# Blending per-sample FFN weights in a fused attention and FFN layer: finer loads, two accumulators, and another place for the second weight matrix

## The chip, the cores and the metric

The kernel runs on 8 cores of one Trainium2 chip. There is no traffic between the cores: each takes one half (2048 positions of 4096) of one of four samples and its own copy of all weights. The time is device microseconds of the slowest core.

## The reference, cut to what matters

```python
xn = _layernorm(x)                       # x: (4, 4096, 1024)
x = x + attn(xn) + ffn(xn)               # windowed attention, 8 heads of 128, window 16

def _L0_ffn_ref(hidden_states, ...):     # F = 4096, H = 1024, E = 8
    h = relu(x @ gate_w1.T + gate_b1)
    g = (h @ gate_w2.T + gate_b2).mean(axis=1)              # (4, 8): one row a sample
    mW1 = W1 + einsum('be,efh->bfh', g, TW1)                # TW1: (8, 4096, 1024) f32
    mb1 = b1 + g @ Tb1
    mW2 = W2 + einsum('be,ehf->bhf', g, TW2)                # TW2: (8, 1024, 4096) f32
    mb2 = b2 + g @ Tb2
    u = gelu(einsum('bsh,bfh->bsf', x, mW1) + mb1)
    return einsum('bsf,bhf->bsh', u, mW2) + mb2
```

Each sample has its own blended weights. So each core adds eight float32 matrices of 16 MB, each times a scalar, to W1, and eight more to W2, before it can use either.

## The kernel before

Every instruction goes through small helpers of a class `Ctx` (so the profile gives one line for all matmuls, L74, one for all ACT operations, L85, one for all VectorE operations, L90, and one for all DMAs, L95). The program is written as one list of steps; each engine runs through it and keeps its own instructions in that order. `cx.wait_at(engine, semaphore, count)` makes one engine wait for a count that was noted when the awaited work was written; `cx.wait(engine, semaphores)` waits for everything on these semaphores written so far. DMAs are issued by the engine named in `cx.dma(q, ...)`, in the order in which they stand there, and a wait in front of a DMA holds up all that is behind it on that engine.

The steps, in order:

1. `emit_ln_gate` and `emit_g`: layer norm of all 4096 positions (written to `xnd` in HBM), the gate, and the eight blend factors `gbc`.
2. `emit_attn`: four chunks of 512 positions. A chunk starts with Q, K and V (`emit_qkv`), then has four tiles of 128 queries (`emit_attn_tile`). In a tile VectorE takes two reciprocals (`rz`), scales the probabilities (`exps`, `expsh`), and adds the residual (`xattn`, in the trace O_s<-pC and O_s<-pD); PE and ACT work in between, each in turn.
3. The builds (`emit_build_group`). Blended W1 (`m1d`) and W2 (`m2d`) are made in 64 groups of 128 rows x 1024: groups 0 to 31 are W1, 32 to 63 are W2. A group loads a 512 KB piece of W into the accumulator `accv` and eight 512 KB pieces of TW into `twv`, which has room for four. VectorE does eight multiply-adds (SCALAR_TENSOR_TENSOR) of 128x1024, the last of which writes bf16 into `mwov`, and a DMA takes that to HBM. TW comes in two transfers of four pieces (2 MB); the second overwrites the first, so it waits for the fourth multiply-add, and the next group's loads wait for the eighth. All of it is issued by SP. After each tile but the first stand three groups (line 533); the 19 that are left stand behind the attention (line 952).
4. `emit_ffn`: four chunks (`sc`) of 512 positions. In its first stage PE multiplies with blended W1 in eight blocks (`fb`), each loaded transposed from `m1d` by eight DMAs of SP, and ACT writes gelu to `u`. In its second stage it multiplies with blended W2 in 32 steps (`ft`), each with one transposed load from `m2d`. Before a block or a step SP waits until the groups that it needs are written (`wait_group_out`). The first matmul of the second stage has this line ahead of it:

```python
                if ft == 0:
                    cx.wait("tensor", "a", "v")
```

Of the kernel before, what the change touches and what calls it, by code (L numbers as in the profile page):

```python
# [10 lines left out]
F32 = mybir.dt.float32  # L11
BF16 = mybir.dt.bfloat16
AF = mybir.ActivationFunctionType
ALU = mybir.AluOpType
BF = ml_dtypes.bfloat16

B, T, D = 4, 4096, 1024
# [18 lines left out]
    "d_mb",  # L36
# [64 lines left out]
def build_program():  # L101
# [38 lines left out]
    s = {}  # L140
    for n, sh, dt in [
# [25 lines left out]
        ("accv", (128, D), F32), ("mwov", (128, D), BF16),  # L167
    ]:
# [45 lines left out]
    bk = {}  # L214
# [196 lines left out]
    def build_lane(g):  # L411
        return "vector"

    def emit_build_group(cx, g):
# [4 lines left out]
        osem = "d_mwo" if lane == "vector" else "d_mwop"
        oq = "sync" if lane == "vector" else "gpsimd"  # L420
        if g < 32:
# [21 lines left out]
        cx.dma(q, twb[:, 0:nper * D].rearrange("p (e d) -> p e d", d=D),
               twsrc[0:nper].rearrange("e f d -> f e d"), dsem)
        cx.wait_at(lane, "a", bk["gbc_a"])
        cx.wait(lane, dsem)
        for e in range(8):
            if e > 0 and e % nper == 0:
                cx.wait_at(q, eng_sem, cx.cnt[eng_sem])
                cx.dma(q, twb[:, 0:nper * D].rearrange("p (e d) -> p e d", d=D),  # L450
                       twsrc[e:e + nper].rearrange("e f d -> f e d"), dsem)
                cx.wait(lane, dsem)
            tw = twb[:, (e % nper) * D:((e % nper) + 1) * D]
            if e > 0:
                cx.wait(lane, "v" if lane == "vector" else "p")
            out = acc if e < 7 else outbuf
            if e == 7:
                po = bk["prev_out"].get(lane)
                if po is not None:
                    cx.wait_at(lane, osem, po)  # L460
            cx.vop("scalar_tensor_tensor", out, tw, s["gbc"][:, e:e + 1], acc,
                   op0=ALU.mult, op1=ALU.add, who=lane)
        bk["build_done"][g] = cx.cnt[eng_sem]
        bk["prev_lane"][lane] = g
        cx.wait_at(oq, eng_sem, bk["build_done"][g])
        cx.dma(oq, dst, outbuf, osem)
        bk["prev_out"][lane] = cx.cnt[osem]
        bk["group_out"][g] = (cx.cnt["d_mwo"], cx.cnt["d_mwop"])

    def emit_vector_builds(cx, n):  # L470
        done = 0
        g = bk["vq"]
        while done < n and g < 64:
            if build_lane(g) == "vector":
                emit_build_group(cx, g)
                done += 1
            g += 1
        bk["vq"] = g

    def emit_pool_builds(cx):  # L480
        for g in range(64):
            if build_lane(g) == "gpsimd":
                emit_build_group(cx, g)

    def emit_attn(cx):
# [4 lines left out]
        emit_pool_builds(cx)  # L490
        for ci in range(NCH):
# [28 lines left out]
            for j in range(NT):  # L520
# [11 lines left out]
                if gt >= 1:  # L532
                    emit_vector_builds(cx, 3)
# [240 lines left out]
    def emit_ffn(cx):  # L774
# [3 lines left out]
        for sc in range(NFC):  # L778
# [8 lines left out]
            for fb in range(8):  # L787
                bpar = fb % 2
# [31 lines left out]
            bk["xtf_war"] = cx.cnt["t"]  # L820
            banksets = [(pA, pB), (pC, pD), (pE0, pE1),
# [120 lines left out]
    def full_schedule(cx):  # L942
        emit_p0(cx)
        if PHASES >= 2:
            emit_ln_gate(cx)
        bk["pa_end_v"] = cx.cnt["v"]
        bk["pa_end_a"] = cx.cnt["a"]
        if PHASES >= 3:
            emit_g(cx)
        if PHASES >= 4:  # L950
            emit_attn(cx)
            emit_vector_builds(cx, 64)
        if PHASES >= 5:
            emit_ffn(cx)
            cx.wait("scalar", "d_out0", "d_out1")
        else:
            emit_dummy_out(cx)

    with nc.Block() as block:
        def run_for(name):  # L960
            def body(eng):
# [4 lines left out]
                    "build_done": {}, "prev_lane": {}, "prev_out": {}, "group_out": {},  # L966
# [111 lines left out]
```

How the kernel before makes its waits and increments, by code:

```python
    def inc(self, sname, instr, k=1):  # L57
        if instr is not None:
            instr.then_inc(self.sems[sname], k)
        self.cnt[sname] += k
# [1 line left out]
    def wait(self, who, *ss):  # L62
        if self.on(who):
            for sname in ss:
                if self.cnt[sname] > 0:
                    self.eng.wait_ge(self.sems[sname], self.cnt[sname])
# [1 line left out]
    def wait_at(self, who, sname, val):  # L68
        if self.on(who) and val > 0:
            self.eng.wait_ge(self.sems[sname], val)
```

## Time and profile before

| | us |
|---|---|
| median of 2 runs | 4000.21 (3997.89 to 4002.54) |
| the profiled execution, its own time | 4010.51 |
| its span on the slowest core (core 5) | 4008.7 |
| spans of the 8 cores | 3947.0 to 4008.7 |
| busy in the span: PE / VectorE (DVE) / ACT | 1178.3 / 971.2 / 365.9 |

No engine is busy for a third of the span. So the busy shares don't name what bounds the kernel, and the waits, the chain that ended last and the timeline have to. The span is cut by steps: 0 to 717 us are step 1 and the first Q, K and V, 717 to 2583 us attention tiles with their builds and three more rounds of Q, K and V, 2583 to 3160 us builds alone, and 3160 to 4009 us the FFN.

### The profile page before, as it was taken

What the parts mean: (1) busy time and instruction counts of PE and PEld (TensorE: products, weight loads), DVE (VectorE), ACT (ScalarE), POOL (GpSimd) and SP (SyncE); (2) the same over time, 40 slices, a digit from 0 to 9 for tenths busy, and PEclk for the clock granted to TensorE, in tenths of its full rate; (3) what the DMA queues carried; (4) which work ended last, traced back from release to release, by engine and by line L of the source; (5) the groups of instructions that cost most, each with busy time, mean ns of one, the idle gap of its engine ahead of it and who ended that gap; (6) DMA issues with size and microseconds to landing.
All of it is one profiled execution on the core that took longest, in us unless ns stands there. A gap on an engine that the chain in (4) does not pass through costs nothing.

```text
span 4008.7 us, 16002 instructions; the slowest of 8 cores (3947.0 to 4008.7 us)
## 1 busy us (share of the span) xinstructions
PE 1178.3 (29%) x5044; PEld 479.3 (12%) x5044; DVE 971.2 (24%) x943; ACT 365.9 (9%) x755; POOL 5.5 (0%) x11
## 2 busy tenths in 40 slices
PE   0433425411251112411134111000000175747475
PEld 0111102200020000200011000000000022213131
DVE  1111111344224442244422433333333200000000
ACT  0111102100120001200011000000000010102020
POOL 0000000000000000000000000000000000000000
PEclk9766768655675556755577555555555598888888
DMA  9132230145314442144521444444445445464644
GB/s 178 50 83 76 53 53 7 68 159 160 114 59 161 160 163 108 61 160 160 171 100 60 150 141 139 158 162 177 159 160 173 121 92 121 93 123 89 124 92 105
DMA packets 459878, 475.20 MB, mean 119 GB/s; under 512 B 356435, under 2 KB 356819, under 8 KB 459668
## 3 DMA queue, kind: packets, MB, share of 16 engines
q1 hardware_dynamic: 384996, 408.28, 33.6%
q10 hardware_dynamic: 70320, 55.40, 5.4%
q0 software_dynamic: 4480, 10.50, 1.7%
q8 instruction: 42, 0.69, 0.1%
q14 instruction: 40, 0.33, 0.0%
HBM read 357.91 MB, written 42.01 MB: 100 GB/s over the span
## 4 chain that ended last, share of the span: by engine, by line
DMA 36%; DVE 22%; PE 22%; SPq 6%; ACT 5%; issue 5%; ACTq 3%; DVEq 0%
DMA O_s<-TW 25%; DVE accv_s L90 14%; SPq L95 6%; DMA O_s<-m2d 6%; PE pA L74 5%; PE pB L74 4%; PE pC L74 4%; PE pU L74 3%; PE pD L74 3%; DVE rz_s L90 3%; ACTq L95 3%; PE pE L74 2%; DMA O_s<-xad 2%; DVE mwov_s L90 2%; DMA xnd<-xnb_s 1%
## 5 line engine op out<-in xcount | busy, mean ns | idle before, releaser
L90 DVE SCALAR_TENSOR_TENSOR accv_s<-O_s,gbc_s,accv_s 128x1024 f32<-128x1024 f32 x448 | 575.1, 1284 | 1102.2 <-DMA O_s<-TW 1068.1
L74 PE MATMUL pA<-O_s 128*128 128x512 bf16 x640 | 197.4, 430 | 965.8 <-DMA O_s<-m1d 758.0
L74 PE MATMUL pU<-rz_s,e0f_s 128*128 128x512 f32 x64 | 58.5, 1070 | 897.9 <-DVE rz_s L90 897.9
L74 PEld LDWEIGHTS pA<-O_s 128*128 128x128 bf16 x640 | 65.7, 106 | 1102.2 <-issue 1058.4
L90 DVE TENSOR_TENSOR O_s<-pA,O_s 128x512 f32<-128x512 f32 x4 | 2.8, 691 | 745.2 <-PE pU L74 745.2
L74 PE MATMUL pB<-O_s 128*128 128x512 bf16 x640 | 181.4, 400 | 0.0
L74 PEld LDWEIGHTS pU<-rz_s,e0f_s 128*128 128x128 f32 x64 | 18.8, 324 | 917.5 <-issue 917.5
L90 DVE RECIPROCAL rz_s<-pE 1x512 f32<-1x512 f32 x32 | 104.8, 3312 | 71.0 <-PE pE L74 71.0
L85 ACT ACTIVATE yt_s<-pU 128x128 bf16<-128x128 f32 x128 | 23.4, 305 | 1048.3 <-PE pU L74 1048.3
L74 PE MATMUL pC<-gb1r_s,e0bf_s 128*128 128x512 bf16 x32 | 13.9, 435 | 350.0 <-DMA xt_s<-xnd 343.2
L90 DVE TENSOR_SCALAR_CACHE_REDUCE junk_s<-O_s 128x1024 f32<-128x1024 f32 x32 | 38.8, 1214 | 319.9 <-ACT hrelu_s L85 319.4
L74 PE MATMUL pE<-O_s 128*128 128x512 bf16 (+1 forms) x384 | 108.4, 337 | 0.0
L85 ACT ACTIVATE O_s<-pA,mb_s 128x512 bf16<-128x512 f32 x64 | 44.0, 687 | 539.2 <-PE pA L74 539.2
L74 PE MATMUL pA<-xt_s,O_s 128*128 128x512 bf16 (+1 forms) x288 | 71.0, 394 | 50.9 <-DMA xt_s<-xnd 44.3
L90 DVE SCALAR_TENSOR_TENSOR mwov_s<-O_s,gbc_s,accv_s 128x1024 bf16<-128x1024 f32 x64 | 82.2, 1285 | 11.0 <-DVE accv_s L90 10.9
L74 PE MATMUL pC<-O_s,xt_s 128*128 128x512 bf16 x256 | 78.6, 462 | 0.0
L74 PE MATMUL pA<-O_s,selbf_s 128*32 128x512 bf16 x15 | 6.4, 428 | 244.7 <-DVE O_s L90 244.7
L74 PE MATMUL pU<-O_s 128*128 128x512 bf16 x256 | 78.3, 388 | 0.0
L74 PEld LDWEIGHTS pB<-O_s 128*128 128x128 bf16 x640 | 66.3, 104 | 75.8 <-issue 23.7
L85 ACT ACT_TABLE_LOAD x2 | 2.6, 1283 | 742.5 <-PE pA L74 696.4
L74 PE MATMUL pC<-O_s,yt_s 128*128 128x512 bf16 x128 | 56.7, 623 | 27.3 <-ACT yt_s L85 27.3
L74 PE MATMUL pD<-O_s 128*128 128x512 bf16 (+1 forms) x192 | 64.6, 336 | 0.0
(135 smaller groups left out, 1335.5 us busy)
## 6 DMA issues: line engine op xcount, KB each, us to landing
O_s<-TW SPq DMA_DIRECT2D x128, 2048.0 KB, 8.5
accv_s<-W SPq DMA_DIRECT2D x64, 512.0 KB, 4.1
O_s<-x SPq DMA_DIRECT2D x16, 1024.0 KB, 7.1
xnd<-xnb_s ACTq DMA_DIRECT2D x32, 256.0 KB, 3.6
O_s<-x ACTq DMA_DIRECT2D x16, 512.0 KB, 3.8
xad<-O_s ACTq DMA_DIRECT2D x16, 512.0 KB, 3.0
m1d<-mwov_s SPq DMA_DIRECT2D x32, 256.0 KB, 2.2
m2d<-mwov_s SPq DMA_DIRECT2D x32, 256.0 KB, 3.4
```

What stands on the lines that cost most here:

```text
L74: i = self.eng.matmul(out, lhsT, rhs, start=start, stop=stop, skip_group_check=skip)
L85: i = self.eng.activation(out, in_, func, **kw) if self.on("scalar") else None
L90: i = getattr(self.eng, name)(*args, **kw) if self.on(who) else None
L95: i = self.eng.dma_start(out=out, in_=in_, transpose=transpose)
```

## The change

- There are four slots for TW, each with a semaphore of its own (`d_ts0` to `d_ts3`). TW comes in eight transfers of 512 KB, one a slot; the load of a slot waits only for the multiply-add that read the slot last. Each multiply-add waits for its own slot.
- There are two accumulators and two output buffers (`accv2` and `mwov2` are new), taken in turn. The load of W waits for the last group but one.
- The write of a group is issued behind its loads and ahead of the next group's, after the eighth multiply-add, on the same engine.
- Behind each tile stand two groups instead of three, and only of W1: 30 in all. The last two of W1 stand in the first FFN chunk ahead of its blocks 0 and 1. All 32 of W2 stand between the first and the second stage of that chunk, and their DMAs are issued by ACT, not SP. They go by columns first: all eight row blocks of one quarter of the columns, then the next quarter.

```diff
+    BLD_ORDER = list(range(32)) + [32 + ht * 4 + fq
+                                   for fq in range(4) for ht in range(8)]
...
     def emit_build_group(cx, g):
...
+        m1 = g < 32
+        q = "sync" if m1 else "scalar"
...
-        prevg = bk["prev_lane"].get(lane)
-        if prevg is not None:
-            cx.wait_at(q, eng_sem, bk["build_done"][prevg])
...
-        cx.dma(q, acc, wsrc, dsem)
-        cx.dma(q, twb[:, 0:nper * D].rearrange("p (e d) -> p e d", d=D),
-               twsrc[0:nper].rearrange("e f d -> f e d"), dsem)
-        cx.wait_at(lane, "a", bk["gbc_a"])
-        cx.wait(lane, dsem)
+        par = bk["bld_n"] % 2
+        acc = s["accv"] if par == 0 else s["accv2"]
+        outbuf = s["mwov"] if par == 0 else s["mwov2"]
+        wdsem = "d_tw" if par == 0 else "d_twp"
+        osem = "d_mwo" if par == 0 else "d_mwop"
+        slots = [s["twv"][:, r * D:(r + 1) * D] for r in range(4)]
+        cx.wait_at(q, "v", bk["acc_done"][par])
+        cx.dma(q, acc, wsrc, wdsem)
...
         for e in range(8):
-            if e > 0 and e % nper == 0:
-                cx.wait_at(q, eng_sem, cx.cnt[eng_sem])
-                cx.dma(q, twb[:, 0:nper * D].rearrange("p (e d) -> p e d", d=D),
-                       twsrc[e:e + nper].rearrange("e f d -> f e d"), dsem)
-                cx.wait(lane, dsem)
...
+            i = i0 + e
+            r = i % 4
...
+            elif e < 4:
+                cx.wait_at(q, "v", bk["mac_cnt"][i - 4])
+            else:
+                cx.wait_at(q, "v", v0 + (e - 4) + 1)
+            ssem = "d_ts%d" % r
+            cx.dma(q, slots[r], twsrc[e], ssem)
+            bk["slot_dma"][i] = (ssem, cx.cnt[ssem])
+        for e in range(8):
+            i = i0 + e
+            ds, dc = bk["slot_dma"][i]
+            cx.wait_at("vector", ds, dc)
...
+            cx.vop("scalar_tensor_tensor", out, slots[i % 4],
+                   s["gbc"][:, e:e + 1], acc, op0=ALU.mult, op1=ALU.add)
...
+        cx.wait_at(q, "v", done)
+        cx.dma(q, dst, outbuf, osem)
...
                 if gt >= 1:
-                    emit_vector_builds(cx, 3)
+                    emit_vector_builds(cx, 2, only_m1=True)
...
             for fb in range(8):
+                if sc == 0:
+                    emit_vector_builds(cx, 1, only_m1=True)
                 bpar = fb % 2
...
             bk["xtf_war"] = cx.cnt["t"]
+            if sc == 0:
+                emit_vector_builds(cx, 64)
             banksets = [(pA, pB), (pC, pD), (pE0, pE1),
...
             emit_attn(cx)
-            emit_vector_builds(cx, 64)
         if PHASES >= 5:
             emit_ffn(cx)
```

What SP issues for the first builds before the change (accv is the accumulator, O_s<-TW a load into the slots, m1d<-mwov_s the write of a group of W1; "waits v" is a wait for VectorE):

```order
L95 DMA m2row_s<-mbd 1x1024 [waits d_mb]
L95 DMA accv_s<-W 128x1024 [waits v,a]
L95 DMA O_s<-TW 128x4x1024
L95 DMA O_s<-TW 128x4x1024 [waits v]
L95 DMA m1d<-mwov_s 128x1024 [waits v]
L95 DMA accv_s<-W 128x1024 [waits v]
L95 DMA O_s<-TW 128x4x1024
```

And after it:

```order
L95 DMA m2row_s<-mbd 1x1024 [waits d_mb]
L95 DMA accv_s<-W 128x1024
L95 DMA O_s<-TW 128x1024 [waits v,a] x4
L95 DMA O_s<-TW 128x1024 [waits v] x4
L95 DMA m1d<-mwov_s 128x1024 [waits v]
L95 DMA accv_s<-W 128x1024
L95 DMA O_s<-TW 128x1024 [waits v] x8
L95 DMA m1d<-mwov_s 128x1024 [waits v]
```

The two transfers of 2 MB have become eight of 512 KB with a wait for each, and the write of a group still stands, with its wait for VectorE, ahead of all loads of the next.

What ACT has at the end of the first stage of the first FFN chunk before the change (O_s<-pA,mb_s is a gelu, O_s<-xad the load of the attention's result for the last addition):

```order
L85 ACTIVATE O_s<-pB,mb_s 128x512 [waits t]
L85 ACTIVATE O_s<-pA,mb_s 128x512 [waits t]
L85 ACTIVATE O_s<-pB,mb_s 128x512 [waits t]
L95 DMA O_s<-xad 128x1024 [waits d_xa0,v]
L95 DMA out<-O_s 128x1024 [waits v]
```

And after it:

```order
L85 ACTIVATE O_s<-pA,mb_s 128x512 [waits t]
L85 ACTIVATE O_s<-pB,mb_s 128x512 [waits t]
L95 DMA accv_s<-W 128x1024 [waits v]
L95 DMA O_s<-TW 128x1024 [waits v] x8
L95 DMA m2d<-mwov_s 128x1024 [waits v]
L95 DMA accv_s<-W 128x1024 [waits v]
L95 DMA O_s<-TW 128x1024 [waits v] x8
```

The loads of W2's 32 groups stand behind the last gelu of the chunk's first stage, and ahead of the loads for its last addition.

What SP has after the change between the last write of the attention's builds and the second block of the first FFN chunk (O_s<-xnd is the transposed input, O_s<-m1d a block of blended W1):

```order
L95 DMA m1d<-mwov_s 128x1024 [waits v]
L95 DMA_TRANSPOSE O_s<-xnd 128x512 [waits t]
L95 DMA_TRANSPOSE O_s<-xnd 128x512 x7
L95 DMA accv_s<-W 128x1024 [waits v]
L95 DMA O_s<-TW 128x1024 [waits v] x8
L95 DMA m1d<-mwov_s 128x1024 [waits v]
L95 DMA_TRANSPOSE O_s<-m1d 128x512 [waits d_mwo,d_mwop,t]
L95 DMA_TRANSPOSE O_s<-m1d 128x512 x7
L95 DMA accv_s<-W 128x1024 [waits v]
L95 DMA O_s<-TW 128x1024 [waits v] x8
L95 DMA m1d<-mwov_s 128x1024 [waits v]
L95 DMA_TRANSPOSE O_s<-m1d 128x512 [waits d_mwo,d_mwop]
```

Before, all builds had been issued by then, and the rows O_s<-m1d stood right behind O_s<-xnd. Now one group stands ahead of the first block and one ahead of the second.

PE's order is the same in both. Its first matmul of the second stage waits for `v` and `a` as counted at that point of the program; after the change the 32 groups of W2 are counted there too:

```order
L74 MATMUL pB<-O_s 128x512 [waits a]
L74 MATMUL pB<-O_s 128x512 x7
L74 MATMUL pA<-m2rowb_s,e0bf_s 128x512 [waits d_m20,a,v]
L74 MATMUL pB<-m2rowb_s,e0bf_s 128x512
L74 MATMUL pC<-m2rowb_s,e0bf_s 128x512
```

## Rows read from the trace of the kernel before

**Rows 1.** The page: span, chain that ended last by engine and by line.

```profile
span 4008.7 us, 16002 instructions; the slowest of 8 cores (3947.0 to 4008.7 us)
...
DMA 36%; DVE 22%; PE 22%; SPq 6%; ACT 5%; issue 5%; ACTq 3%; DVEq 0%
DMA O_s<-TW 25%; DVE accv_s L90 14%; SPq L95 6%; DMA O_s<-m2d 6%; PE pA L74 5%; PE pB L74 4%; PE pC L74 4%; PE pU L74 3%; PE pD L74 3%; DVE rz_s L90 3%; ACTq L95 3%; PE pE L74 2%; DMA O_s<-xad 2%; DVE mwov_s L90 2%; DMA xnd<-xnb_s 1%
```

**Rows 2.** Busy time in stretches of the span: us, busy by engine, PEclk, DMA share, GB/s.

```profile
core 5: us, PE busy (x) PEld busy (x) DVE busy (x) ACT busy (x) POOL busy (x), PEclk, DMA share, GB/s
...
717.00:1046.00 329.00, 60.31 (x264) 27.00 (x262) 128.12 (x100) 15.13 (x50) 0.00 (x0) 0.57 0.40 141
...
2583.00:3160.00 577.00, 0.00 (x0) 0.00 (x0) 195.33 (x153) 0.00 (x0) 0.00 (x0) 0.50 0.47 164
3160.00:3376.00 216.00, 130.82 (x520) 51.40 (x520) 2.58 (x4) 23.27 (x33) 0.00 (x0) 0.86 0.49 98
```

**Rows 3.** Timeline of one attention tile: start us, us, engine, line, operation.

```profile
1350.81 6.55 DVE L90 RECIPROCAL rz_s<-pE 1x512 f32<-1x512 f32 x2
...
1373.44 0.68 DVE L90 TENSOR_TENSOR O_s<-pD,O_s 128x512 f32<-128x512 f32 x1
1374.04 5.44 DVE L90 SCALAR_TENSOR_TENSOR accv_s<-O_s,gbc_s,accv_s 128x1024 f32<-128x1024 f32 x4
...
1379.56 0.38 SPq L95 DMA_DIRECT2D O_s<-TW  x1
...
1381.60 0.31 PE L74 MATMUL pE<-expsh_s,ohalbf_s 128*1 128x128 bf16 x1
1387.76 4.06 DVE L90 SCALAR_TENSOR_TENSOR accv_s<-O_s,gbc_s,accv_s 128x1024 f32<-128x1024 f32 x3 [8.28 <-DMA O_s<-TW]
1392.00 1.28 DVE L90 SCALAR_TENSOR_TENSOR mwov_s<-O_s,gbc_s,accv_s 128x1024 bf16<-128x1024 f32 x1 [0.17 <-DVE accv_s L90]
1393.36 0.36 SPq L95 DMA_DIRECT2D m1d<-mwov_s  x1
...
1394.24 14.92 SPq L95 DMA_DIRECT2D O_s<-TW  x2
1403.25 5.45 DVE L90 SCALAR_TENSOR_TENSOR accv_s<-O_s,gbc_s,accv_s 128x1024 f32<-128x1024 f32 x4 [9.97 <-DMA O_s<-TW]
```

**Rows 4.** Groups of VectorE instructions from 770 to 2584 us: the 45 groups beside attention.

```profile
L90 DVE SCALAR_TENSOR_TENSOR accv_s<-O_s,gbc_s,accv_s 128x1024 f32<-128x1024 f32 x315 | 404.3, 1284 | 724.0 <-DMA O_s<-TW 699.7 <-DVE accv_s L90 0.9
...
L90 DVE SCALAR_TENSOR_TENSOR mwov_s<-O_s,gbc_s,accv_s 128x1024 bf16<-128x1024 f32 x45 | 57.8, 1285 | 7.7 <-DVE accv_s L90 7.6
```

**Rows 5.** The chain that ended last, in order of time: start us, us, what.

```profile
2408.12 14.43 DMA O_s<-TW
2428.17 10.45 DMA O_s<-TW
...
2977.38 10.54 DMA O_s<-TW
2993.54 8.20 DMA O_s<-TW
```

**Rows 6.** The page's DMA issues: KB each, median us from issue to landing.

```profile
O_s<-x ACTq DMA_DIRECT2D x16, 512.0 KB, 3.8
```

**Rows 7.** Timeline of the start of the FFN, PE and SP.

```profile
3160.41 10.13 SPq L95 DMA_TRANSPOSE O_s<-xnd  x8
3170.70 87.57 SPq L95 DMA_TRANSPOSE O_s<-m1d  x64
3184.34 3.57 PE L74 MATMUL pA<-O_s 128*128 128x512 bf16 x8 [686.49 <-DMA O_s<-m1d]
...
3206.77 3.57 PE L74 MATMUL pA<-O_s 128*128 128x512 bf16 x8 [5.79 <-DMA O_s<-m1d]
...
3217.96 1.89 PE L74 MATMUL pA<-O_s 128*128 128x512 bf16 x8 [2.42 <-DMA O_s<-m1d]
...
3268.60 0.38 PE L74 MATMUL pA<-m2rowb_s,e0bf_s 128*128 128x512 bf16 x1 [1.14 <-ACT O_s L85]
```

More of the change, by code:

```diff
@@ L35 @@
     "d_xr0", "d_xr1", "d_xa0", "d_xa1", "d_xf0", "d_xf1", "d_out0", "d_out1",
-    "d_mb",
[1 row of a table added]
     "t", "v", "a", "p",
@@ L167, in build_program @@
         ("accv", (128, D), F32), ("mwov", (128, D), BF16),
+        ("accv2", (128, D), F32), ("mwov2", (128, D), BF16),
     ]:
@@ L445, in emit_build_group @@
-        cx.wait_at(lane, "a", bk["gbc_a"])
-        cx.wait(lane, dsem)
-        for e in range(8):
-            if e > 0 and e % nper == 0:
-                cx.wait_at(q, eng_sem, cx.cnt[eng_sem])
-                cx.dma(q, twb[:, 0:nper * D].rearrange("p (e d) -> p e d", d=D),
-                       twsrc[e:e + nper].rearrange("e f d -> f e d"), dsem)
-                cx.wait(lane, dsem)
-            tw = twb[:, (e % nper) * D:((e % nper) + 1) * D]
-            if e > 0:
-                cx.wait(lane, "v" if lane == "vector" else "p")
-            out = acc if e < 7 else outbuf
[L457 to L462, printed above, removed]
@@ new lines, in emit_build_group @@
+        cx.wait_at(q, "v", bk["acc_done"][par])
+        cx.dma(q, acc, wsrc, wdsem)
+        wsem, wcnt = wdsem, cx.cnt[wdsem]
+        i0 = bk["bld_idx"]
+        v0 = cx.cnt["v"]
+        for e in range(8):
+            i = i0 + e
+            r = i % 4
+            if i < 4:
+                cx.wait_at(q, "v", bk["pa_end_v"])
+                cx.wait_at(q, "a", bk["pa_end_a"])
+            elif e < 4:
[5 more added lines that the diff above has]
+            bk["slot_dma"][i] = (ssem, cx.cnt[ssem])
@@ new lines, in emit_build_group @@
+        for e in range(8):
+            i = i0 + e
+            ds, dc = bk["slot_dma"][i]
+            cx.wait_at("vector", ds, dc)
+            if e == 0:
+                cx.wait_at("vector", wsem, wcnt)
+                cx.wait_at("vector", "a", bk["gbc_a"])
+            cx.wait("vector", "v")
+            out = acc if e < 7 else outbuf
+            if e == 7 and bk["out_sem"][par] is not None:
+                osm, ocn = bk["out_sem"][par]
+                cx.wait_at("vector", osm, ocn)
+            cx.vop("scalar_tensor_tensor", out, slots[i % 4],
+                   s["gbc"][:, e:e + 1], acc, op0=ALU.mult, op1=ALU.add)
+            bk["mac_cnt"][i] = cx.cnt["v"]
@@ L468, in emit_build_group, with emit_vector_builds @@
+        bk["bld_idx"] = i0 + 8
+        done = cx.cnt["v"]
+        bk["acc_done"][par] = done
+        cx.wait_at(q, "v", done)
+        cx.dma(q, dst, outbuf, osem)
+        bk["out_sem"][par] = (osem, cx.cnt[osem])
+        bk["bld_n"] += 1
         bk["group_out"][g] = (cx.cnt["d_mwo"], cx.cnt["d_mwop"])
-    def emit_vector_builds(cx, n):
+    def emit_vector_builds(cx, n, only_m1=False):
         done = 0
[L472 to L483, printed above, removed]
+        while done < n and bk["vq"] < 64:
+            if only_m1 and BLD_ORDER[bk["vq"]] >= 32:
+                return
+            emit_build_group(cx, BLD_ORDER[bk["vq"]])
+            bk["vq"] += 1
+            done += 1
     def emit_attn(cx):
@@ L489, in emit_attn @@
         bk["kt_war"] = bk["g_done_t"]
-        emit_pool_builds(cx)
         for ci in range(NCH):
@@ L965, in body @@
                     "relu_a": [], "hbar_t": [], "xt_gate_t": [],
-                    "build_done": {}, "prev_lane": {}, "prev_out": {}, "group_out": {},
+                    "group_out": {},
+                    "bld_n": 0, "bld_idx": 0, "slot_dma": {}, "mac_cnt": {},
+                    "acc_done": {0: 0, 1: 0}, "out_sem": {0: None, 1: None},
                     "vq": 0, "hraw_a": [], "qraw_a": [], "kstt_v": [], "ppa": [],
```

22 lines of the change are left out of this document (1 added, 21 removed), and 1 row of the table SEM_NAMES.

## The prediction

> **What bounds the kernel now.** I read the page first. The chain that ended last is 36% DMA and 22% VectorE; its two longest entries are the loads of TW, 25%, and the multiply-adds on the accumulator, 14% [rows 1]. That is the build of the blended weights. The stretches then show where it stands alone: from 2583 to 3160 us PE and ACT do nothing, VectorE is busy 195 of 577 us and the DMA engines 0.47 of the time at 164 GB/s [rows 2]. So neither engine is full; they take turns. The timeline shows how. The first four multiply-adds end at 1379.5, the next load goes out at 1379.56, VectorE idles 8.28 us, works 5.5 us, the write goes out at 1393.36, and the next multiply-add starts at 1403.25 [rows 3]. A group of W1 is 9.9 + 5.5 + 8.3 + 5.5, some 29.3 us, of which 11 are work. In the stretch with builds alone, all W2, it is 577 / 19 = 30.4.
>
> Attention does not cover this. A tile's own part, from the reciprocals at 1350.81 to the residual at 1374.04, needs VectorE in between and takes 23.2 us [rows 3]. PE has the next tile ready at about 1381.9, 8 us later, and waits for VectorE, which has builds for another 70. So each group's time is added to the tile's. The 45 groups in attention cost 404.3 + 724.0 + 57.8 + 7.7 = 1193.8 us, busy and idle together [rows 4]: 79.6 a tile, less than three times 29.3 since the first group's loads land during the tile's own part. The last 19 cost 577 us. Together 1771 of 4010.5 us.
>
> **A group after the change.** The write still stands between two groups on the issuing engine, behind the wait for the eighth multiply-add. So four slots are not refilled across the border: at each border nothing is in flight, and write, W and four TW loads go out together, with the same bytes as now. They land as now: 9.9 us from the write's issue to the fourth slot [rows 3]. The gain is behind that. The fifth load goes out when the first multiply-add is done, long before the fourth slot lands, and comes right behind it in the stream. A load of 512 KB takes 3.8 us [rows 6], one of 2 MB 7.8 us (1379.56 to 1387.76, less the waits for semaphores and the start) [rows 3]: the three further pieces cost 1.33 us each. After that VectorE sets the pace. Today multiply-adds stand 1.39 us apart with one wait, and 1.46 us where there are two (three take 4.06 us, the one after them starts 4.24 us after the first; 4.24 - 2 x 1.39) [rows 3]; now all have two. So a group of W1 is 9.9 + 1.3 + 4 x 1.46 = 17.1 us, and one of W2 1.1 more (30.4 - 29.3), 18.2.
>
> The rate is the doubtful part, since each core will ask for 280 GB/s where it asked for 164. The first bound is 1.33 us a slot. The other comes from 164 GB/s at a DMA share of 0.47 [rows 2]: full engines would move 349 GB/s, 1.50 us for 512 KB. I take the middle, 1.41. Six slots' worth of bytes stand in a row at a border, so 6 x 0.09, some 0.55 us a group: 17.65 for W1 and 18.75 for W2.
>
> Here a page speaks. The Trainium skill, HBM Reference, Specifications, says that two cores share a memory stack, a core alone reaches some 425 GB/s and each of two about 358. By that an estimate is 1.46 us a slot when both stream, and the sum below would be some 15 us higher. No row here shows one core against its neighbour.
>
> The first group of a tile finds W and four pieces landed, as now (four multiply-adds follow 1374.04 at once) [rows 3]. Its fifth piece goes out after the first multiply-add and lands 3.8 us later, when the fourth ends. So it is 8 x 1.46 = 11.7 us. The 23.2 us of the tile's own part cover the 9.9 us; without that cover it would be 17.65.
>
> **The parts of the sum.**
> - Attention: 15 tiles x (11.7 + 17.65) = 440 us instead of 1193.8: -753.5. The next tile is ready 8 us after the builds begin, so 29 us of builds still hide that. The 23.2 us and the three rounds of Q, K and V stay. I give nothing for a warmer PE: its granted clock is 0.57 in these stretches [rows 2] since it idles for some 70 us in every tile, and it would still idle 20 us; after a gap of only 5.79 us it has fallen to the lower level (8 matmuls in 3.57 us), after 2.42 us it has not (1.89 us) [rows 7].
> - The last two groups of W1: on SP they stand behind the transposed input (10.3 us) and ahead of blocks 0 and 1. Now the first block comes 23.9 us after 3160.41, of which 13.6 from its own issue [rows 7]. After: 10.3 + 17.2 + 0.45 + 13.6 = 41.6, 17.7 later. Behind the block's eight issues (10 us) comes the second group and then block 1: 28 + 10 + 17.65 + 13.6 = 69.3, against 46.4 now. Queued behind is only SP's own list; PE and ACT wait for it. Together +23.
> - W2: 32 groups x 18.75 = 600 us instead of the 577 us of the 19 that stood alone: +23. They start when ACT has issued its last gelu. Nothing lies beside them. Their order by columns suggests that the second stage should overlap with them, but its first matmul waits for VectorE's count with all 32 in it, where it now waits only for a gelu (idle 1.14 us at 3268.60) [rows 7]. Behind them on ACT's queue are the loads for the last addition, which are not due yet.
> - The second accumulator and output buffer: nothing. The write is behind the wait for the group's end in any case, and W's load lands ahead of the first slot. No instruction is added but the issues, 0.38 us each [rows 3], six more a group; they run under the transfers.
> - The rest of the FFN stays: three chunks and the second stage of the first.
>
> 4010.5 - 753.5 + 23 + 23 = 3303 us against the profiled execution. That one is 10 us above the median of the runs, 4000.2, so I take 8 off: **3295 us**, -17.6%. A microsecond a group is worth 15 + 2 + 32 = 49 us.
>
> **Rivals.**
> - *The loads stream at full rate across the whole group.* If the fixed part of a landing overlapped even at the border, a group would be its 4.98 MB at 349 GB/s, 14.3 us: 15 x 26 = 390, 32 x 14.3 = 458, the two of W1 +16, in all 4010.5 - 804 - 119 + 16 = 3103. For it: the DMA engines have room. Against: the write and its wait in front of all loads of the next group, in the order of the program.
> - *The memory gives out.* Between 2408 and 2439 us two transfers took 14.43 and 10.45 us instead of 10.54 and 8.20 [rows 5], at less than half load. At that price throughout, 5.5 + 2.6 more than the 8.9 and 7.8 of rows 3, a group of W1 would be 25 us, the sum 3666. Half of that extra, 4 us a group, gives 3470. For it: all eight cores now read harder, W2 in pieces of rows far apart. Against: later transfers of the same kind are short again.
> - *Small loads are paid singly* (this is the one that ends above the time before). If each of the nine loads cost its 3.8 us [rows 6] with no overlap with the one ahead on the queue, a group would be 0.4 + 9 x 3.8 + 1.5 = 36.1 us and the first of a tile 18.2: 15 x 54.3 = 815, 32 x 36.1 = 1155, +60 for the two of W1, 4010.5 - 379 + 578 + 60 = 4270 us. It becomes slower by 2% from 32.4 us a group. Against it: write, W and the 2 MB behind them are all issued between 1393.36 and 1394.24 and have landed by 1403.25, 9.9 us; W and the 2 MB singly would be 3.8 + 7.8 = 11.6 without the write [rows 3, 6].
> - *The second stage does overlap with W2.* Then three quarters of some 100 us (3268.60 to 3376) go: 3220. The wait named above speaks against it.
>
> A page speaks for the third rival. The Trainium skill, DMA: Bandwidth & Descriptors, Measured, asks for transfers of at least 1 MiB, and puts a single one at 2.0 us and its bytes at 436 GB/s; its estimate for 512 KB is 3.2 us. Paid singly, that makes 30.7 us a group and a time of about 4005, no gain. The same page says that the fixed part is mostly the wait for completion, which need not hold up the next transfer, and the row on W and the 2 MB agrees.
>
> **How the numbers follow.** Forecast (groups of 16.5 to 19.5 us, 3230 to 3380): 0.62. Memory gives out: 0.19. Full stream: 0.12. Overlap of the second stage: 0.03. Small loads singly: 0.04, half of it above +2%. The range reaches to the full stream and to half the extra of the slow transfers: 3110 to 3480. Within 2% is what a measurement of this kernel can hardly tell from no change; only the third rival and halves of it get there. Faster 0.97, same 0.01, slower 0.02.
>
> **What would show it.** After the change: groups behind the first of a tile 17 to 18 us from write to write, with VectorE idle some 6 us before the first multiply-add and then 1.3 to 1.5 us between starts; first groups 11 to 12 us; a tile 52 to 53 us from reciprocal to reciprocal instead of 99; W2's groups about 600 us with PE idle all through; PE's first matmul of the second stage released by VectorE; the FFN's last three chunks as before. I am wrong if landing times of single slots climb with load (then W2's groups show it first), if VectorE idles before each multiply-add rather than at borders, or if PE has matmuls between W2's groups.

## The result and the profile after

The changed kernel takes 3491.6 us (median of 11 runs, 3482.07 to 3508.78) against 4000.0 (10 runs): a ratio of 0.873, 95% interval 0.871 to 0.875. A few executions of any kernel here are some per cent slow on one half of the chip; the ratios, and the medians of the experiments below, leave those out. The forecast was 3295, with a range from 3110 to 3480. The direction, what bounds the kernel and where the gain lies were right; the saving is 508 us instead of 705, and the time lies 12 us above the range.

The page of the kernel after, its span and the chain that ended last, by engine and line (the answer to [rows 1]), and its loads (the answer to [rows 6]: KB each, median us from issue to landing):

```profile
span 3495.8 us, 17506 instructions; the slowest of 8 cores (3407.8 to 3495.8 us)
...
DMA 34%; PE 26%; DVE 18%; ACT 6%; issue 6%; SPq 6%; ACTq 4%; DVEq 1%
DMA O_s<-TW 21%; DVE accv_s L90 9%; DMA O_s<-m2d 6%; PE pA L74 6%; SPq L95 6%; PE pB L74 5%; PE pC L74 5%; PE pU L74 4%; ACTq L95 4%; PE pD L74 4%; DVE rz_s L90 3%; PE pE L74 2%; DMA O_s<-xad 2%; DVE mwov_s L90 2%; DMA xnd<-xnb_s 2%
...
O_s<-TW SPq DMA_DIRECT2D x256, 512.0 KB, 5.8
O_s<-TW ACTq DMA_DIRECT2D x256, 512.0 KB, 6.9
accv_s<-W SPq DMA_DIRECT2D x32, 512.0 KB, 4.1
accv_s<-W ACTq DMA_DIRECT2D x32, 512.0 KB, 5.5
...
O_s<-x ACTq DMA_DIRECT2D x16, 512.0 KB, 4.0
```

The loads of TW are still the largest entry. A single 512 KB transfer that stands alone, O_s<-x, takes 4.0 us, against 3.8 before. The same amount as a slot's load takes 5.8 us for W1 (SP's queue) and 6.9 us for W2 (ACT's).

One tile with its two groups of W1, VectorE and SP (the answer to [rows 3]):

```profile
1069.26 6.55 DVE L90 RECIPROCAL rz_s<-pE 1x512 f32<-1x512 f32 x2
...
1092.10 0.68 DVE L90 TENSOR_TENSOR O_s<-pD,O_s 128x512 f32<-128x512 f32 x1
1092.89 5.45 DVE L90 SCALAR_TENSOR_TENSOR accv_s<-O_s,gbc_s,accv_s 128x1024 f32<-128x1024 f32 x4
1099.53 1.28 DVE L90 SCALAR_TENSOR_TENSOR accv_s<-O_s,gbc_s,accv_s 128x1024 f32<-128x1024 f32 x1 [1.19 <-DMA O_s<-TW]
1101.72 1.28 DVE L90 SCALAR_TENSOR_TENSOR accv_s<-O_s,gbc_s,accv_s 128x1024 f32<-128x1024 f32 x1 [0.91 <-DMA O_s<-TW]
1103.74 1.28 DVE L90 SCALAR_TENSOR_TENSOR accv_s<-O_s,gbc_s,accv_s 128x1024 f32<-128x1024 f32 x1 [0.74 <-DMA O_s<-TW]
1105.20 1.28 DVE L90 SCALAR_TENSOR_TENSOR mwov_s<-O_s,gbc_s,accv_s 128x1024 bf16<-128x1024 f32 x1 [0.17 <-DVE accv_s L90]
1106.56 0.34 SPq L95 DMA_DIRECT2D m1d<-mwov_s  x1
...
1107.47 12.31 SPq L95 DMA_DIRECT2D O_s<-TW  x8
1113.92 5.45 DVE L90 SCALAR_TENSOR_TENSOR accv_s<-O_s,gbc_s,accv_s 128x1024 f32<-128x1024 f32 x4 [7.44 <-DMA O_s<-TW]
1119.70 1.28 DVE L90 SCALAR_TENSOR_TENSOR accv_s<-O_s,gbc_s,accv_s 128x1024 f32<-128x1024 f32 x1 [0.33 <-DMA O_s<-TW]
...
1125.31 1.28 DVE L90 SCALAR_TENSOR_TENSOR mwov_s<-O_s,gbc_s,accv_s 128x1024 bf16<-128x1024 f32 x1 [0.17 <-DVE accv_s L90]
1126.51 6.55 DVE L90 RECIPROCAL rz_s<-pE 1x512 f32<-1x512 f32 x2
```

The shape is the one in the prediction. The first group of the tile starts at once with four multiply-adds; then the fifth piece is late by 1.2 us, and the group ends 13.7 us after its start instead of 11.7 (1092.89 to the write at 1106.56). At the border the write goes out at 1106.56 and the next multiply-add starts at 1113.92, 7.4 us later, and the fifth at 1119.70, 13.1 us after the write instead of 11.2. The whole second group is 20.1 us, from 1106.56 to the write at 1126.66. The tile is 57.3 us where 52 to 53 were expected.

The groups of VectorE instructions over the whole of attention's builds (the answer to [rows 4]), 30 groups:

```profile
L90 DVE SCALAR_TENSOR_TENSOR accv_s<-O_s,gbc_s,accv_s 128x1024 f32<-128x1024 f32 x210 | 269.7, 1284 | 185.5 <-DMA O_s<-TW 171.2 <-DVE accv_s L90 0.5
...
L90 DVE SCALAR_TENSOR_TENSOR mwov_s<-O_s,gbc_s,accv_s 128x1024 bf16<-128x1024 f32 x30 | 38.5, 1285 | 7.6 <-DVE accv_s L90 3.9 <-DMA O_s<-TW 3.6
```

Busy and idle together make 501 us, 33.4 a tile, where 440 us were forecast.

A group of W2, from the write before it:

```profile
2318.15 0.35 ACTq L95 DMA_DIRECT2D m2d<-mwov_s  x1
...
2319.07 12.53 ACTq L95 DMA_DIRECT2D O_s<-TW  x8
2325.73 5.45 DVE L90 SCALAR_TENSOR_TENSOR accv_s<-O_s,gbc_s,accv_s 128x1024 f32<-128x1024 f32 x4 [7.66 <-DMA O_s<-TW]
2332.77 1.28 DVE L90 SCALAR_TENSOR_TENSOR accv_s<-O_s,gbc_s,accv_s 128x1024 f32<-128x1024 f32 x1 [1.58 <-DMA O_s<-TW]
2335.20 1.28 DVE L90 SCALAR_TENSOR_TENSOR accv_s<-O_s,gbc_s,accv_s 128x1024 f32<-128x1024 f32 x1 [1.15 <-DMA O_s<-TW]
2336.91 1.28 DVE L90 SCALAR_TENSOR_TENSOR accv_s<-O_s,gbc_s,accv_s 128x1024 f32<-128x1024 f32 x1 [0.43 <-DMA O_s<-TW]
2338.37 1.28 DVE L90 SCALAR_TENSOR_TENSOR mwov_s<-O_s,gbc_s,accv_s 128x1024 bf16<-128x1024 f32 x1 [0.17 <-DVE accv_s L90]
2339.74 0.35 ACTq L95 DMA_DIRECT2D m2d<-mwov_s  x1
```

The fifth load can go out when the first multiply-add ends, 2327.0, and its multiply-add starts at 2332.77, 5.8 us later. I had given 3.8 us to that load. That is one half of what a group costs too much; the other lies at the border. Averaged over 28 of W2's groups on this core (timeline, 2060 to 2740 us), VectorE idles 8.4 us between the last multiply-add of a group and the first of the next, where some 6 were forecast, and takes 13.9 us from there to the group's end, where 8 x 1.46 = 11.7 were. At the end of these groups PE starts, released by VectorE, as the wait for its count says:

```profile
2752.22 0.59 PE L74 MATMUL pA<-m2rowb_s,e0bf_s 128*128 128x512 bf16 x1 [708.51 <-DVE mwov_s L90]
```

### The profile page after: what moved, and what is told of

Same layout as the page of the kernel before. It is cut to its first block, busy times and chain, and to the rows that moved or that the text cites. A ratio compares the mean times of both kernels' runs of the same rounds, so it can differ in the third digit from the quotient of the medians.

```text
span 3495.8 us, 17506 instructions; the slowest of 8 cores (3407.8 to 3495.8 us)
## 1 busy us (share of the span) xinstructions
PE 1206.6 (35%) x5044; PEld 487.1 (14%) x5044; DVE 972.7 (28%) x943; ACT 365.9 (10%) x755; POOL 5.5 (0%) x11
## 4 chain that ended last, share of the span: by engine, by line
DMA 34%; PE 26%; DVE 18%; ACT 6%; issue 6%; SPq 6%; ACTq 4%; DVEq 1%
DMA O_s<-TW 21%; DVE accv_s L90 9%; DMA O_s<-m2d 6%; PE pA L74 6%; SPq L95 6%; PE pB L74 5%; PE pC L74 5%; PE pU L74 4%; ACTq L95 4%; PE pD L74 4%; DVE rz_s L90 3%; PE pE L74 2%; DMA O_s<-xad 2%; DVE mwov_s L90 2%; DMA xnd<-xnb_s 2%
## 5 line engine op out<-in xcount | busy, mean ns | idle before, releaser
L74 PE MATMUL pC<-gb1r_s,e0bf_s 128*128 128x512 bf16 x32 | 14.3, 448 | 342.5 <-DMA xt_s<-xnd 335.7
L74 PE MATMUL pC<-O_s,xt_s 128*128 128x512 bf16 x256 | 85.7, 495 | 0.0
L74 PEld LDWEIGHTS pU<-rz_s,e0f_s 128*128 128x128 f32 x64 | 18.8, 324 | 401.1 <-issue 401.1
L90 DVE SCALAR_TENSOR_TENSOR O_s<-raw_s,qwc_s,rbq_s 128x512 bf16<-128x512 f32 x32 | 21.6, 746 | 163.7 <-ACT rbq_s L85 163.7
```

What stands on the lines that cost most here:

```text
L74: i = self.eng.matmul(out, lhsT, rhs, start=start, stop=stop, skip_group_check=skip)
L90: i = getattr(self.eng, name)(*args, **kw) if self.on(who) else None
```

## The experiments

The price of a group below is read from one view: a stretch in which VectorE does nothing but multiply-adds, its length divided by the count in brackets behind VectorE's busy time, times eight. The columns are the stretch, its length, busy time (x count) of PE, PE's weight loads, VectorE, ACT and POOL, the granted clock, the DMA share and GB/s. For the kernel before it is the row 2583:3160 of [rows 2]: 577 / 153 x 8 = 30.2 us, DMA share 0.47 at 164 GB/s. For the kernel after, W2's groups, 600 / 216 x 8 = 22.2 us:

```profile
2100.00:2700.00 600.00, 0.00 (x0) 0.00 (x0) 275.17 (x216) 0.00 (x0) 0.00 (x0) 0.50 0.73 224
```

All of these rows are of the slowest core of their run. The same view on the other cores of this execution gives 20.7 us on cores 0 and 1 and 21.5 to 22.2 on the rest, so a few tenths between two runs mean little.

My theory at this point ("load"): the slots' landings grow because other cores read at the same time. The rival ("singly"): each 512 KB transfer costs something on its own queue, whoever else reads.

### One core, two cores

The edit, for the kernel after and for the kernel before (2 in the place of 1 for two cores); the cores that don't run leave their part of the output to a copy of core 0's or 1's:

```diff
+    in_maps = in_maps[:1]
-    res = run_bass_kernel_spmd(nc, in_maps, core_ids=list(range(8)))
+    res = run_bass_kernel_spmd(nc, in_maps, core_ids=list(range(1)))
...
-        out[b, t * OWN:(t + 1) * OWN] = np.asarray(res.results[core]["out"])
+        out[b, t * OWN:(t + 1) * OWN] = np.asarray(res.results[core % 1]["out"])
```

The changed kernel on one core:

> The changed kernel on one core, seven cores idle; the output of that core stands for all. Theory 'load': a slot lands late because the other cores read at the same time. Then TW's median landing on ACT's queue falls from 6.9 us to 5 or less, a group of W2 from 22.1 to 17 to 18.5 us, and the span to about 3300 us. Theory 'singly': each 512 KB transfer pays something of its own on its queue, whoever else reads. Then landing 6.5 to 7, groups 21 to 22 us, span 3440 or more.

On two cores:

> The changed kernel on two cores, 0 and 1. If neighbours share what is short, groups of W2 are as slow as with eight cores (21 to 22 us, span 3400 to 3490). If what is short is shared by the whole chip, they are as fast as with one core (17 to 18.5 us, about 3300). Theory 'singly': no difference between one, two and eight.

The kernel before on one core:

> The kernel before on one core. Theory 'load': half as hard a reader gains less: a group of W2 goes from 30.4 to 28 to 29 us, landing of 2 MB from 8.5 to 8, span 3880 to 3940. Theory 'singly': unchanged, 3980 to 4010.

Measured: 3314.6 us on one core, 3511.7 on two, 3491.6 on eight. The kernel before on one core: 3921.6. The page's DMA issues of the changed kernel on one core:

```profile
O_s<-TW SPq DMA_DIRECT2D x256, 512.0 KB, 5.1
O_s<-TW ACTq DMA_DIRECT2D x256, 512.0 KB, 5.5
```

ACT's slots land after 5.5 us instead of 6.9, not after 5 or less as the theory had it. The lone load O_s<-x takes 3.5 us on this core, so more than half of what a slot's load takes beyond a lone one is there without any neighbour. W2's groups with one core, then with two, then the kernel before with one:

```profile
2050.00:2600.00 550.00, 0.00 (x0) 0.00 (x0) 290.76 (x227) 0.00 (x0) 0.00 (x0) 0.50 0.75 257
```

```profile
2100.00:2740.00 640.00, 0.00 (x0) 0.00 (x0) 294.96 (x231) 0.00 (x0) 0.00 (x0) 0.50 0.74 226
```

```profile
2560.00:3100.00 540.00, 0.00 (x0) 0.00 (x0) 184.86 (x144) 0.00 (x0) 0.00 (x0) 0.50 0.48 165
```

A group of W2 costs 19.4 us with one core, 22.2 with two (22.4 on core 0) and 20.7 to 22.2 with eight. The one-core figure misses the 17 to 18.5 that was expected, and 3511.7 us lies above the 3490. But the whole rise from 19.4 comes with the first neighbour, and the six other cores add nothing that shows: cores 0 and 1 share what is short. "Singly" falls as the cause of that rise, though not of the 19.4 itself. Why the same pair paid 22.2 to 22.4 in one execution and 20.7 in the other stays open, and no run puts core 0 beside a core that is not its neighbour.

For core 0, alone and with core 1, the timelines give by stage: 39 us more to the end of attention (1851.7 to 1890.3), 92 us more for W2's 32 groups (617 to 709), 32 us more behind them (699 to 731). So of the 168 us between the two spans (3312.9 and 3481.3) somewhat over half is W2's groups, and the neighbour costs something in every stage. The kernel before is 2% faster when alone, but its groups of W2 are 540 / 144 x 8 = 30.0 us there against 30.2, where I had expected 28 to 29, and its 2 MB transfers land after 8.5 us in both: it waits for one transfer at a time, and a neighbour hardly mattered in that stretch. What it gains lies elsewhere, and part of it is only that core 0 is set against the slowest of eight: core 0 itself had a span of 3947.0 us in the profiled execution before, 27 more than the 3919.8 alone, and 24 of these lie ahead of its first tile (reciprocals at 710.4 and 686.6 us).

The Trainium skill, HBM Reference, Specifications, says that the two cores of a pair share one memory stack. The pattern of one, two and eight cores (19.4, 22.2, 20.7 to 22.2 us) agrees.

### The new loads alone, the new places alone

`slots_only` has the new loads in the old places:

```diff
-        q = "sync" if m1 else "scalar"
+        q = "sync"
...
-    BLD_ORDER = list(range(32)) + [32 + ht * 4 + fq
-                                   for fq in range(4) for ht in range(8)]
+    BLD_ORDER = list(range(64))
...
-                    emit_vector_builds(cx, 2, only_m1=True)
+                    emit_vector_builds(cx, 3)
...
-                if sc == 0:
-                    emit_vector_builds(cx, 1, only_m1=True)
...
-            if sc == 0:
-                emit_vector_builds(cx, 64)
...
             emit_attn(cx)
+            emit_vector_builds(cx, 64)
```

> The new loads (four slots, two accumulators) in the old places: three groups a tile, 19 behind the attention, all issued by SP, rows of W2 in the old order. By the prices of the changed kernel's profile (first group of a tile 13.6 us, a further one 20 us, W2 22 us): 45 groups in attention 15 x (13.6 + 40.2) = 807 instead of 1194, 19 groups 420 instead of 577, so about 3460 to 3490 us, level with the changed kernel: the move is worth nothing. Rival: ACT's queue or the order by columns makes W2 slow; then the 19 groups take 20 us or less each and the whole 3400 to 3440.

`move_only` has the new places with the old loads and one accumulator:

```diff
-        cx.dma(q, acc, wsrc, wdsem)
...
-            cx.dma(q, slots[r], twsrc[e], ssem)
...
+        cx.dma(q, acc, wsrc, "d_tw")
+        cx.dma(q, twb[:, 0:nper * D].rearrange("p (e d) -> p e d", d=D),
+               twsrc[0:nper].rearrange("e f d -> f e d"), "d_tw")
...
+            if e == nper:
+                cx.wait_at(q, "v", cx.cnt["v"])
+                cx.dma(q, twb[:, 0:nper * D].rearrange("p (e d) -> p e d", d=D),
+                       twsrc[e:e + nper].rearrange("e f d -> f e d"), "d_tw")
```

> The new places (two groups of W1 a tile, two in the FFN, 32 of W2 by ACT's queue, by columns) with the old loads, one accumulator, two transfers of 2 MB. By the prices of before: 15 x (21.5 + 29.3) = 762 instead of 1194, two groups in the FFN +45, 32 x 30.4 = 973 instead of 577: 4010 to 4030 us, no change. Rival: ACT's queue or the order by columns costs by itself, then 4060 or more; or saves, 3960 or less.

Measured: `slots_only` 3511.2 us, ratio to before 0.874 (0.868 to 0.879), the interval of the whole change (0.871 to 0.875) inside it. `move_only` 4021.1 us, ratio 1.005 (1.002 to 1.007), inside the 4010 to 4030 expected; `slots_only` is above its 3460 to 3490. All of the gain is the loads; the move gives nothing, since a group costs much the same in either place. `slots_only` has the second accumulator and output buffer too. That they add nothing, as the prediction says, was not tried. The stretches with W2's groups alone, `slots_only` first:

```profile
2250.00:2660.00 410.00, 0.00 (x0) 0.00 (x0) 193.75 (x151) 0.00 (x0) 0.00 (x0) 0.50 0.74 231
```

```profile
2500.00:3200.00 700.00, 0.00 (x0) 0.00 (x0) 233.99 (x183) 0.00 (x0) 0.00 (x0) 0.50 0.46 161
```

On SP's queue, in the old order, a group of W2 is 410 / 151 x 8 = 21.7 us. So ACT's queue and the order by columns account for some 0.5 us of the 22.2, less than the cores differ among themselves, and the rival about them (20 us or less) falls. With the old loads a group is 700 / 183 x 8 = 30.6, in the new place as in the old.

### The write behind the next loads

`write_behind` keeps all, but holds the write of a group back until W and the first four TW loads of the next are issued (the edit is cut; the last write of a stretch, which has no next group, is sent by a second helper):

```diff
+            if e == 3 and pend is not None:
+                flush_write(cx, pend)
...
-        cx.wait_at(q, "v", done)
-        cx.dma(q, dst, outbuf, osem)
-        bk["out_sem"][par] = (osem, cx.cnt[osem])
+        bk["pend"] = (q, done, dst, outbuf, osem, par, g)
...
+    def flush_write(cx, pend):
+        q, done, dst, outbuf, osem, par, g = pend
+        cx.wait_at(q, "v", done)
+        cx.dma(q, dst, outbuf, osem)
+        bk["out_sem"][par] = (osem, cx.cnt[osem])
+        bk["group_out"][g] = (cx.cnt["d_mwo"], cx.cnt["d_mwop"])
```

> The write of a group moves behind the W and the first four TW loads of the next, so the slots are refilled across the border. Theory 'latency': the neighbour makes each landing longer, but there is room to have more in flight; then the 7.5 us before a group's first multiply-add shrink, a group of W2 goes from 22 to 18.5 to 20 us and the second group of a tile from 20 to 16.5 to 18; 3330 to 3400 us. Rival 'ceiling': two neighbours get no more than the 2 x 225 GB/s that they have; then W2's groups stay at 21 to 22 us, landings grow, only the tiles gain a little, 3450 to 3490.

And on one core:

> The same on one core. Theory 'latency' and 'ceiling' both expect it well below the 3314.6 us of the changed kernel on one core: groups of W2 15 to 16.5 us, span about 3200. If it stays above 3280, the border was not what cost the 7 us.

Measured: 3350.5 us on eight cores (two runs), ratio to before 0.836 (0.831 to 0.841), so 141 less than the kernel after, and 3116.3 on one. W2's groups with eight cores, then with one:

```profile
2080.00:2600.00 520.00, 0.00 (x0) 0.00 (x0) 280.16 (x219) 0.00 (x0) 0.00 (x0) 0.50 0.93 262
```

```profile
2000.00:2400.00 400.00, 0.00 (x0) 0.00 (x0) 281.10 (x220) 0.00 (x0) 0.00 (x0) 0.50 0.97 343
```

That is 19.0 us with eight and 14.5 us with one core: on one core the DMA engines are full (0.97) and the group costs the 14.3 us that the prediction's "full stream" gave from the share and the rate of before. That is better than the 15 to 16.5 expected. With a neighbour they are busy too (0.93) and move only 262 GB/s: each packet takes longer. The rival "ceiling" at 2 x 225 GB/s falls. Whether 2 x 262 is a limit for W2's rows isn't shown. It is none for the core: in the same execution, beside attention and with W1's rows, it moved 360 GB/s from 1120 to 1130 us, though what its neighbour read at that moment isn't known. The timeline on one core at a border (write issued 2217.98):

```profile
2216.20 1.28 DVE L90 SCALAR_TENSOR_TENSOR mwov_s<-O_s,gbc_s,accv_s 128x1024 bf16<-128x1024 f32 x1 [1.01 <-DMA O_s<-TW]
2217.98 0.40 ACTq L95 DMA_DIRECT2D m2d<-mwov_s  x1
2218.77 4.06 DVE L90 SCALAR_TENSOR_TENSOR accv_s<-O_s,gbc_s,accv_s 128x1024 f32<-128x1024 f32 x3 [1.29 <-DMA O_s<-TW]
```

The first multiply-add of the next group starts 2.6 us after the last of this one, where it took 8.9 in the kernel after on eight cores (2316.79 to 2325.73). Like with like, the idle time at the border falls from 6.9 to 1.2 us on average on one core, and from 8.4 to 1.5 with eight. So the write in front of the loads is what drained the slots, as the prediction had it.

### Rows of W2 and of W1

`w2_contig` lets the 32 groups that stand for W2 read W1 and TW1, whose rows of 4 KB follow each other, where W2's are 16 KB apart. W2's blend is left out; bytes, number and writes of the groups are the same.

```diff
-            wsrc = ap["W2"][ht * 128:(ht + 1) * 128, fq * D:(fq + 1) * D]
-            twsrc = ap["TW2"][:, ht * 128:(ht + 1) * 128, fq * D:(fq + 1) * D]
+            gg = g - 32
+            wsrc = ap["W1"][gg * 128:(gg + 1) * 128, :]
+            twsrc = ap["TW1"][:, gg * 128:(gg + 1) * 128, :]
```

> The changed kernel, but the 32 groups that stand for W2 read W1's and TW1's rows (4 KB rows one behind the other instead of 16 KB apart); so W2's blend is left out and W1's is written in its place, and the time alone counts. If neighbours disturb each other by rows far apart, these groups fall from 22.2 us to 19 to 20.5 and the whole to 3400 to 3440. If it is the amount of bytes alone, they stay at 21.5 to 22.5 and the whole at 3480 to 3500.

And on one core:

> The kernel with W1's rows in the place of W2's (W2's blend left out) on one core. A group of that kind took 19.9 us with eight cores, one of real W2 22.2 with eight and 19.3 with one. If the rows' distance matters only between neighbours, it is level with real W2 on one core, 19 to 19.5 us. If it costs something by itself too, it is at W1's own price on one core, 18.0 to 18.5, and the whole 3275 to 3290.

Measured: 3442.7 us on eight cores (ratio 0.859, 0.853 to 0.865), 49 less than the changed kernel, and 3293.9 on one, 21 less. Both lie 3 to 4 us above what was expected. The groups with eight cores, then with one:

```profile
2100.00:2650.00 550.00, 0.00 (x0) 0.00 (x0) 283.84 (x222) 0.00 (x0) 0.00 (x0) 0.50 0.75 251
```

```profile
2050.00:2550.00 500.00, 0.00 (x0) 0.00 (x0) 273.09 (x213) 0.00 (x0) 0.00 (x0) 0.50 0.77 263
```

| a group, us | one core | eight cores, the slowest | the neighbour's part |
|---|---|---|---|
| rows 16 KB apart | 19.4 | 22.2 | 2.8 |
| rows one behind the other | 18.8 | 19.8 | 1.0 |

The amount read is the same in both lines. By the length of the whole stage divided by 32, all eight cores lie at 20.7 to 22.1 us in the first line and at 19.7 to 20.2 in the second, medians 21.9 and 19.9. The two don't overlap. So the neighbour's part is not set by bytes alone: by the medians somewhat over half of it, by the slowest cores two thirds, comes with the rows' distance, which by itself costs 0.6 us. (On core 0, where the first line was lowest, it is 20.7 against 19.8, hardly more than alone: how much the neighbour adds differs from pair to pair and from execution to execution.) As to the expectation of the last run, both answers hold in part: 18.8 lies between the two, and so does the whole. That where the bytes lie matters so much speaks for the memory itself as the shared thing, rather than for queues or engines. That is argued, not shown, and which part of the memory was not tried.

### PE's wait, and builds under Q, K and V

`pe_early` gives the first matmul of the second stage in chunk 0 the count of VectorE at the end of attention:

```diff
-                if ft == 0:
+                if ft == 0 and sc == 0:
+                    cx.wait("tensor", "a")
+                    cx.wait_at("tensor", "v", attn_v)
+                elif ft == 0:
                     cx.wait("tensor", "a", "v")
```

> PE's first matmul of the second stage of chunk 0 waits for VectorE's count at the end of attention instead of for all 32 groups of W2; nothing else is changed. Three quarters of that stage (95 us, 70) then run beside the builds: 3420 to 3435 us. Rival: the transposed loads beside them slow the builds by as much; then 3470 to 3490 and W2's groups cost 23 us or more.

Measured: 3465.4 us (0.865, 0.860 to 0.870), 26 less than the kernel after, where some 70 were expected. The stretch of W2's groups:

```profile
2150.00:2750.00 600.00, 70.15 (x200) 23.90 (x200) 270.73 (x212) 0.00 (x0) 0.00 (x0) 0.55 0.81 229
```

PE does 70 us of matmuls in it, and after the last build 673 us are left instead of 744: those 70 us came. A group costs 600 / 212 x 8 = 22.6 us instead of 22.2: the transposed loads take their part. All eight cores of the two profiled executions place the rest. On average 663 us instead of 727 follow the last build, 64 less; W2's groups take 713 instead of 691, 21 more; and what lies ahead of them, which the edit does not touch, is 8 longer. The average span is 35 us shorter. So a third of what PE gains is paid back in the builds.

Both edits together:

> Both edits: the write behind the next loads, and the second stage of chunk 0 no longer behind all of W2's groups. The late write gave 112 us and the early PE 26. With W2's groups at 18.9 us the pair of neighbours is nearer to what it can move, so the transposed loads cost as much as PE gains: 3350 to 3380 us. If the two add up, 3350; if the memory is full, 3370 or more.

Measured: 3348.3 us (two runs), 0.835 (0.826 to 0.844), against 3350.5 and 0.836 for the late write alone. The two don't add up. (The expectation took 112 us for the late write where the medians here give 141, so its 3350 is not the sum of the two gains; that would be some 3324.) On cores 4 to 7, with a granted clock of 0.70 to 0.71 in both profiled executions, the part behind W2's groups is 54 us shorter on average (726 to 673), and the groups take 44 us longer (594 to 638).

`in_qkv` has both and puts five groups into each round of Q, K and V, all of attention's builds on SP's queue:

```diff
-                    emit_vector_builds(cx, 2, only_m1=True)
+                    emit_vector_builds(cx, 2)
...
+        rbq_a = cx.cnt["a"]
+        emit_vector_builds(cx, 2)
         cx.wait_at("vector", "t", bk["qt_war"])
-        cx.wait("vector", "a")
+        cx.wait_at("vector", "a", rbq_a)
...
+        rbk_a = cx.cnt["a"]
+        emit_vector_builds(cx, 2)
         cx.wait_at("vector", "t", bk["kt_war"])
-        cx.wait("vector", "a")
+        cx.wait_at("vector", "a", rbk_a)
...
+        emit_vector_builds(cx, 1)
         for j in range(NT):
```

> Both edits, and five groups put in each Q, K and V stage of attention, two before each of VectorE's scaling steps of Q and K and one before V, where VectorE now idles some 80 of 97 us and the DMA share is 0.10. Two groups stay behind each tile; 14 of W2 are left for the FFN instead of 32, and none of W1. 18 x 18.9 us of W2 and some 45 us of W1 go from the path, and each stage grows by 5 to 15 us since two groups (30 us) only just fit under Q and under K: 2960 to 3060 us. If a stage grows by 40 us or more, VectorE's place there was not free, and the result is 3150 or more.

Measured: 3020.7 us (three runs), ratio to before 0.753 (0.746 to 0.760), inside what was expected, and 13% below the changed kernel. A round of Q, K and V with its builds, and one of the kernel before:

```profile
883.00:1012.00 129.00, 61.58 (x250) 23.26 (x250) 76.99 (x75) 31.12 (x52) 0.00 (x0) 0.82 0.90 261
1538.00:1682.00 144.00, 65.89 (x250) 24.55 (x250) 75.34 (x74) 31.11 (x52) 0.00 (x0) 0.77 0.95 225
```

```profile
1046.00:1151.00 105.00, 62.44 (x239) 23.03 (x240) 16.63 (x28) 31.12 (x52) 0.00 (x0) 0.87 0.10 37
```

VectorE does 77 us in such a round instead of 17, and the DMA share is 0.90 instead of 0.10. From the last reciprocals of a chunk to the first of the next it takes 160 us (852.3 to 1012.2) in the first case, against 169 in `write_behind`, which has five groups less there, and 181 (1501.5 to 1682.1) against 157 in the third, where the groups are W2's and the DMA share is 0.95 at 225 GB/s.

## Why the prediction was wrong

- *What bounds the kernel* held: PE in a tile waits for VectorE and VectorE for TW, and each group's time is added. `slots_only` and `move_only` show that the loads are the whole gain.
- *The border* held: nothing is in flight there, and it is the write ahead of the loads that does it (`write_behind`, 22.2 to 19.0 us). Only its length was wrong.
- *The step that failed* is the price of a group, in its two halves. First, "They land as now: 9.9 us" and "The fifth load goes out when the first multiply-add is done, long before the fourth slot lands, and comes right behind it in the stream", with 3.8 us for a load that meets an empty queue and 1.33 us for one in a row. Even on one core a group of W2 is 19.4 us, not 18.2, and a further group of W1 some 18.1, not 17.1. A slot's load lands after 5.1 to 5.5 us there; VectorE idles 6.9 us at the border of W2's groups, not some 6, and takes 12.5 us from there to the end, not 11.7. I had taken the landing of a lone transfer, and the increment from transfers that are one issue. Second, and larger, "six slots' worth x 0.09, some 0.55 us a group" for the rate: the neighbour costs 1.3 to 2.8 us on W2 with eight cores. I took the middle between two rates that were both measured while the cores' DMA engines idled half of the time, and cited the Trainium skill (HBM Reference, Specifications), which says that two cores share the bandwidth, without letting that widen the price. The likeliest case should have been nearer to "the memory gives out", whose half-way price, 3470 us, is 22 us off.
- *The terms, against the sum of 3303* (the profiled execution took 3497.6). Attention's 30 groups cost 501 us instead of 440: +61. From the first transposed load to W2's first load it takes 149 us; before it was 107, so 42 more, and 23 more were forecast: +19. W2's 32 groups last from 2043.9 to 2752.0, 708 us instead of 600: +108. The rest is +7. At 49 us for each us a group, the 2.4 to 3.5 us that a further group was dearer than forecast are the bulk of it.
- *The rivals*: full stream did not come, for the reason given against it, and came at once in `write_behind_1core` at the price given, 14.5 us. Small loads singly: no. Overlap of the second stage: no, PE's first matmul was released by VectorE 0.3 us after the last multiply-add. "The memory gives out" comes nearest to what happened, though not as bouts but as a steady price; that it is the memory is argued from the neighbour and the rows, not shown.
- *No gain for PE's clock* held for the kernel's time (granted clock 0.59 to 0.63 in three tiles' stretches, 0.57 before); *the rest of the FFN stays* held: 744 us from W2's end against 740.
- The one-core time, 3314.6, is near the sum of 3303 partly by chance: the steps ahead of the first tile were 24 us shorter there than before (693.7 against 717.7), and the groups 0.5 to 1 us dearer than forecast.

## What to carry to other kernels

When a change raises the rate at which a core reads, the prices read before it are prices at the old load: take one profile of the kernel with a single core and one with two before trusting them, since here the neighbour alone was worth 168 us on core 0 and the other six nothing that shows. In a queue that issues in order, look at what stands between the last load of one round and the first of the next: a write that waits for the round's end empties all the slots, and moving it behind the next loads gave 141 us. Then look for stretches in which both the engine and the DMA queues idle; five groups under each round of Q, K and V gave 328 us more, over twice as much as the late write.

## What the runs showed of the hardware

- Cores 0 and 1 slow each other and the other six don't: 19.4 us a group with one core, 22.2 and 22.4 with two, 20.7 to 22.2 with eight, at the same number of bytes.
- How far apart the rows lie matters little alone and much with a neighbour: 4 KB rows 16 KB apart cost 0.6 us a group more than rows one behind the other on one core, and 2.0 on eight by the medians of the cores (19.9 to 21.9).
- A core whose queue never ran dry moved 343 GB/s alone at a DMA share of 0.97, and 262 with its neighbour at 0.93. So the DMA share doesn't say how much more can be moved. The Trainium skill, HBM Reference, Specifications, gives about 358 GB/s to each of two; the neighbours here had 262, and the measurement decides.
